# Attend pass of a Performer block: four numerator products gathered at the next group's head, over two banks and two sets of features

## The reference

```
pq  = exp(proj - sq - stab) / sqrt(m) + 1e-06      # features of q
kv  = einsum('bhsm,bhsk->bhmk', pk, v)
z   = sum(pk, axis=2)
num = einsum('bhsm,bhmk->bhsk', pq, kv)
den = einsum('bhsm,bhm->bhs', pq, z)
out = num / den[..., None]
out = out.transpose(...).reshape(...) @ wo
```

## Time and profile before

| | us |
|---|---|
| median of 3 runs | 3307.4 (3306.03 to 3308.24) |
| the profiled execution | 3309.45 |
| its span | 3307.6 |
| PE busy in the span | 3246.5 (98%) |
| DVE, ACT, POOL busy | 2279.7, 1657.2, 1086.0 |
| numerator products L1356, 2048 matmuls | 138.8 busy |
| feature products L1338 and L1344 | 44.3 + 41.2 and 61.4 busy |

### The profile page before, as it was taken

How to read it: one execution, slowest core, us unless ns; L and a number is a source line. 1 busy time by engine, 2 the same in 40 slices (tenths; PEclk the granted TensorE clock), 3 DMA queues, 4 the chain that set the end, 5 groups by cost and what they waited for, 6 DMA issues and landing times.

```text
span 3307.6 us, 73559 instructions
## 1 busy us (share of the span) xinstructions
PE 3246.5 (98%) x28521; PEld 2826.8 (85%) x28521; DVE 2279.7 (69%) x4678; ACT 1657.2 (50%) x3552; POOL 1086.0 (33%) x857
## 2 busy tenths in 40 slices
PE   7999999998899999999999999999999999999998
PEld 6777777777677777777777789999999999999998
DVE  6777777777567667676676666666666676676666
ACT  5666666666454545454545454443444443444443
POOL 3555554555355656565656430000000000000000
PEclk9999999999999999999999999999999999999999
DMA  3222222223344443434434463444444444444443
GB/s 122 95 87 76 102 87 86 95 87 95 105 103 120 109 122 100 129 92 126 111 108 117 137 223 133 146 150 150 147 153 147 151 143 153 139 139 142 150 147 128
DMA packets 250121, 409.60 MB, mean 124 GB/s; under 512 B 94512, under 2 KB 119600, under 8 KB 249776
## 3 DMA queue, kind: packets, MB, share of 16 engines
q1 hardware_dynamic: 249776, 404.90, 38.1%
HBM read 292.50 MB, written 112.33 MB: 122 GB/s over the span
## 4 chain that ended last, share of the span: by engine, by line
PE 72%; DVE 1%; issue 0%; POOL 0%; DMA 0%; ACT 0%; SPq 0%; DVEq 0%; POOLq 0%; ACTq 0%
PE ffn_hidden L188 32%; PE attend_gated L188 22%; PE ffn_result L188 8%; PE attend_num L1356 4%; PE attend_feat L1320 2%; PE attend_feat L1338 2%; PE ffn_turn L1803 1%; PE attend_feat L1344 1%; PE attend_turn L1328 0%; DVE ffn_yb L1770 0%; DMA den_d<-attend_raw 0%; DVE attend_top L1255 0%; DVE attend_below_parts L1268 0%; DVE attend_below_parts L1266 0%; POOL shared_y L1163 0%
## 5 line engine op out<-in xcount | busy, mean ns | idle before, releaser
L188 PE MATMUL ffn_hidden<-ffn_yT_hi,ffn_wa_hi 128*128 128x256 f32 x2048 | 574.1, 280 | 4.9 <-DVE ffn_wa_lo L1691 2.9
L188 PE MATMUL ffn_hidden<-ffn_yT_lo,ffn_wa_hi 128*128 128x256 f32 x2048 | 573.3, 280 | 0.0
L188 PE MATMUL ffn_hidden<-ffn_yT_hi,ffn_wa_lo 128*128 128x256 f32 x2048 | 572.1, 279 | 0.0
L329 POOL TENSOR_TENSOR ffn_n_rstd<-ffn_n_base,ffn_n_power 128x2 f32<-128x2 f32 x32 | 27.5, 860 | 1299.4 <-DVE ffn_n_negmean L324 1299.4
L188 PEld LDWEIGHTS ffn_hidden<-ffn_yT_hi,ffn_wa_hi 128*128 128x128 f32 x2048 | 385.0, 188 | 5.9 <-DVE ffn_wa_lo L1691 3.6
L188 PEld LDWEIGHTS ffn_hidden<-ffn_yT_hi,ffn_wa_lo 128*128 128x128 f32 x2048 | 385.2, 188 | 0.0
L188 PEld LDWEIGHTS ffn_hidden<-ffn_yT_lo,ffn_wa_hi 128*128 128x128 f32 x2048 | 384.9, 188 | 0.2
L1673 ACT ACTIVATE ffn_ht_hi<-ffn_hs 128x512 fp32r<-128x512 f32 x248 | 156.7, 632 | 409.9 <-DVE ffn_hs L1720 409.9
L1724 DVE TENSOR_TENSOR ffn_ht_lo<-ffn_hs,ffn_ht_hi 128x512 fp32r<-128x512 f32 x248 | 173.6, 700 | 219.2 <-ACT ffn_ht_hi L1673 219.2
L698 ACT ACTIVATE keys_e<-keys_feat,keys_below 128x128 f32<-128x128 f32 x1024 | 283.3, 412 | 54.6 <-DVE keys_below L763 54.6
L633 POOL TENSOR_TENSOR keys_z_sum<-keys_z_sum,keys_e 128x512 f32<-128x512 f32 x192 | 243.7, 1287 | 189.9 <-ACT keys_e L698 189.7
(11 more groups left out here) (274 smaller groups left out, 9560.7 us busy)
## 6 DMA issues: line engine op xcount, KB each, us to landing
ffn_tq<-part_d SPq DMA_DIRECT2D x248, 512.0 KB, 4.0
keys_xin<-in_L_attn_x_dram SPq DMA_DIRECT2D x32, 512.0 KB, 4.2
xn_d<-keys_xn SPq DMA_DIRECT2D x32, 512.0 KB, 2.8
xT_d<-keys_xT_whole SPq DMA_DIRECT2D x32, 512.0 KB, 2.6
u_d<-keys_uq_turned SPq DMA_DIRECT2D x32, 512.0 KB, 2.9
shared_xTf<-xT_d SPq DMA_DIRECT2D x32, 512.0 KB, 5.3
r_d<-shared_gate SPq DMA_DIRECT2D x32, 512.0 KB, 3.1
attend_o<-rden_d SPq DMA_DIRECT2D x128, 128.0 KB, 2.7
```

Source lines behind the costliest of these rows:

```text
L188: last = pe.matmul(out, stationary[a], moving[b], start=start and n == 0, stop=stop and n == len(TERMS) - 1)
```

## The change

The four `num` jobs of a group leave the body (where 0, 1 and 2 stood behind `feat` 1, `out` 1 and `wo` 1, and 3 behind the next `max` 0) and stand together at the head of the next group's body, on PE and on ACT. Chunks 0 and 2 go to bank `num`, 1 and 3 to bank `turn`, which otherwise holds the turned `below`. The features of `hi` 1 get tiles of their own, `pT_late`, and `hi` goes ahead of `out` 1 on DVE. In `feat` the four products with `belowT` of the first chunk go behind the second chunk's plain ones. The crossing lists change alike.

```diff
-        pT = [sb(f"pT{j}_hi", [P, 2 * GT]) for j in range(HC)]
+        pT_late = sb("pT_late", [P, HC, 2 * GT])
+        pT = [[sb(f"pT{j}_hi", [P, 2 * GT]) for j in range(HC)], [pT_late[:, j, :] for j in range(HC)]]
...
+        num_bank = [num.t, turn]
...
-        PE_BODY = [("max", 0, 0), ("num", 3, -1), ("k", 0, 0), ("max", 1, 0), ("k", 1, 0), ("r", 0, 0),
...
+        PE_BODY = [("num", 0, -1), ("num", 1, -1), ("num", 2, -1), ("num", 3, -1), ("max", 0, 0), ("k", 0, 0),
...
-                act.activation(raw[:, n, :], num.t[:, :], ACT.Copy).then_inc(num.free, 1)
+                act.activation(raw[:, n, :], num_bank[n % 2][:, :], ACT.Copy).then_inc(num.free, 1)
...
-                        wait(dve, num.full, NC * g + 2 * n)
-                        dve.tensor_scalar(pT[j][:, :], feat[j].t[:, :], FLOOR, None, ALU.add).then_inc(feat[j].free, 1)
+                        wait(dve, num.full, NC * (g - 1) + 2 * n + 2)
+                        dve.tensor_scalar(pT[n][j][:, :], feat[j].t[:, :], FLOOR, None, ALU.add).then_inc(feat[j].free, 1)
...
                 if job == "below":
-                    wait(pe, belowT_ready, g)
+                    wait(pe, num.free, NC * g)
...
                 if job == "feat":
                     for c in range(2):
-                        cols = slice(c * GT, (c + 1) * GT)
                         for j in range(HC):
-                            pe.matmul(feat[j].t[:, cols], omT[rows(j), :], qT[g % 2][rows(j), 2 * n + c, :], start=True, stop=False)
-                        if c == 0 and n == 0:
-                            pe.wait_ge(belowT_ready, g + 1)
...
+                            pe.matmul(feat[j].t[:, c * GT:(c + 1) * GT], omT[rows(j), :], qT[g % 2][rows(j), 2 * n + c, :],
+                                      start=c == 0, stop=False)
+                    pe.wait_ge(belowT_ready, g + 1)
...
+                    for c in range(2):
                         for j in range(HC):
-                            last = pe.matmul(feat[j].t[:, cols], pick[rows(j), 2 * n + c, :], belowT[rows(j), :],
-                                             start=False, stop=True)
+                            last = pe.matmul(feat[j].t[:, c * GT:(c + 1) * GT], pick[rows(j), 2 * n + c, :],
+                                             belowT[rows(j), :], start=False, stop=c == 1)
...
                 if job == "num":
-                        pe.wait_ge(kvz_ready, 2 * b + 2)
-                    wait(pe, num.free, NC * g + n)
+                        pe.wait_ge(kvz_ready, 2 * (g // GB) + 2)
+                    if n == 1:
+                        pe.wait_ge(belowT_ready, g + 1)
+                    wait(pe, num.free, NC * g + n - 1)
...
-                            last = pe.matmul(num.t[rows(j), part * GT:(part + 1) * GT],
+                            last = pe.matmul(num_bank[n % 2][rows(j), part * GT:(part + 1) * GT],
...
-                                             pT[j][:, n % 2 * GT:(n % 2 + 1) * GT], start=True, stop=True)
+                                             pT[n // 2][j][:, n % 2 * GT:(n % 2 + 1) * GT], start=True, stop=True)
```

More of the change, by code:

```diff
@@ L1015, in attend_pass @@
         y_ready, gained, offsets, y_stored = sem("y_ready"), sem("gained"), sem("offsets"), sem("y_stored")
-        PE_BODY = [("max", 0, 0), ("num", 3, -1), ("k", 0, 0), ("max", 1, 0), ("k", 1, 0), ("r", 0, 0),
-                   ("below", 0, 0), ("feat", 0, 0), ("r", 1, 0), ("out", 0, 0), ("feat", 1, 0),
-                   ("num", 0, 0), ("out", 1, 0), ("num", 1, 0), ("wo", 0, -1), ("wo", 1, -1),
-                   ("num", 2, 0)]
-        DVE_BODY = [("top", 0, 0), ("top", 1, 0), ("recip", 0, -1), ("below", 0, 0), ("mix", 0, 1), ("exp", 0, 0), ("o", 0, -1), ("out", 0, 0),
-                    ("out", 1, 0), ("mix", 1, 1), ("hi", 1, 0), ("wo", 0, -1), ("wo", 1, -1),
-                    ("stats", 0, -1),
-                   ("part_lo", 0, 0)]
-        ACT_BODY = [("num", 3, -1), ("norm", 0, -2), ("k", 0, 0), ("k", 1, 0), ("below", 0, 0), ("kv", 0, 0),
-                    ("r", 0, 0), ("exp", 0, 0), ("mix", 0, 1), ("r", 1, 0), ("oT", 0, -1),
-                    ("num", 0, 0), ("exp", 1, 0), ("num", 1, 0), ("mix", 1, 1), ("num", 2, 0),
-                   ("part_hi", 0, 0)]
+        PE_BODY = [("num", 0, -1), ("num", 1, -1), ("num", 2, -1), ("num", 3, -1), ("max", 0, 0), ("k", 0, 0),
+                   ("max", 1, 0), ("k", 1, 0), ("r", 0, 0), ("below", 0, 0), ("feat", 0, 0), ("r", 1, 0), ("out", 0, 0),
+                   ("feat", 1, 0), ("out", 1, 0), ("wo", 0, -1), ("wo", 1, -1)]
+        DVE_BODY = [("top", 0, 0), ("top", 1, 0), ("recip", 0, -1), ("below", 0, 0), ("mix", 0, 1), ("exp", 0, 0),
+                    ("o", 0, -1), ("out", 0, 0), ("hi", 1, 0), ("out", 1, 0), ("mix", 1, 1), ("wo", 0, -1),
+                    ("wo", 1, -1), ("stats", 0, -1), ("part_lo", 0, 0)]
+        ACT_BODY = [("num", 0, -1), ("num", 1, -1), ("num", 2, -1), ("num", 3, -1), ("norm", 0, -2), ("k", 0, 0),
+                    ("k", 1, 0), ("below", 0, 0), ("kv", 0, 0), ("r", 0, 0), ("exp", 0, 0), ("mix", 0, 1), ("r", 1, 0),
+                    ("oT", 0, -1), ("exp", 1, 0), ("mix", 1, 1), ("part_hi", 0, 0)]
         POOL_BODY = [("diff", 0, 1), ("k", 0, 0), ("k", 1, 0), ("norm", 0, -2), ("mix", 0, 1), ("oT", 0, -1),
@@ L1866, in feed_forward_pass @@
         return Programs(sync, gpsimd, scalar, vector, tensor, mem), y_loaded, stored
-PE_CROSSING = (("attend", "max", 0, -1), ("attend", "num", 3, -2), ("attend", "k", 0, -1), ("attend", "max", 1, -1),
-               ("attend", "k", 1, -1), ("attend", "r", 0, -1), ("attend", "below", 0, -1), ("attend", "feat", 0, -1),
-               ("attend", "r", 1, -1), ("attend", "out", 0, -1), ("attend", "num", 0, -1), ("attend", "out", 1, -1),
-               ("attend", "feat", 1, -1), ("attend", "num", 1, -1), ("attend", "wo", 0, -2), ("attend", "num", 2, -1),
-               ("attend", "wo", 1, -2), ("attend", "num", 3, -1), ("ffn", "turn", 0, 0), ("ffn", "w1", 0, 0),
+PE_CROSSING = (("attend", "num", 0, -2), ("attend", "num", 1, -2), ("attend", "num", 2, -2), ("attend", "num", 3, -2),
+               ("attend", "max", 0, -1), ("attend", "k", 0, -1), ("attend", "max", 1, -1), ("attend", "k", 1, -1),
+               ("attend", "r", 0, -1), ("attend", "below", 0, -1), ("attend", "feat", 0, -1), ("attend", "r", 1, -1),
+               ("attend", "out", 0, -1), ("attend", "feat", 1, -1), ("attend", "out", 1, -1), ("attend", "wo", 0, -2),
+               ("attend", "wo", 1, -2), ("attend", "num", 0, -1), ("attend", "num", 1, -1), ("attend", "num", 2, -1),
+               ("attend", "num", 3, -1), ("ffn", "turn", 0, 0), ("ffn", "w1", 0, 0),
                ("ffn", "w1", 1, 0), ("ffn", "w1", 2, 0), ("ffn", "w2", 0, 0), ("ffn", "w2", 1, 0),
@@ L1880 @@
                 ("attend", "below", 0, -1), ("attend", "exp", 0, -1), ("attend", "o", 0, -2),
-                ("attend", "out", 0, -1), ("attend", "out", 1, -1), ("attend", "hi", 1, -1), ("attend", "wo", 0, -2),
+                ("attend", "out", 0, -1), ("attend", "hi", 1, -1), ("attend", "out", 1, -1), ("attend", "wo", 0, -2),
                 ("ffn", "weights", 0, 0), ("attend", "wo", 1, -2), ("attend", "stats", 0, -2), ("ffn", "turn", 0, 0),
```

15 lines of the change are left out of this document (8 added, 7 removed), and 2 rows, old and new, of the table KEYS_OVER.

## The result

The changed kernel takes 3288.27 us in the median of its runs (3284.26 to 3290.12), the kernel before 3307.01 beside it (3306.03 to 3308.24): a ratio of 0.9942 with a 95% interval of 0.9927 to 0.9957. That is 18.7 us less. 3287.0 was predicted.

The account below looks back on a forecast made before the run. The prediction took PE's own work as the bound. It summed 12 us from 30 periods, 4.5 from group 0 and 3.5 from the end to 20 us, forecasting a median of 3287 us (own case 3279 to 3297, range 3270 to 3306).

Parts of the forecast that it names:

- PE's sum: PE's work per group: numerators and `max` 0 0.60 less, `feat` 0.10 less, 0.05 lost on banks; 0.65 us saved.
- the ring: Two numerator banks at the head: `num` 2 waits for ACT's copy to free its bank, 0.05 us lost a group.
- The wait for `oT_lo`: PE at `wo` 0 waits for POOL's `oT_lo`: 0.35 us plus 0.10 restart a group, leaving a gain of 0.20.
- all behind it on POOL end about 0.25 later: With `feat` 0 faster, DVE's `o` goes first and delays POOL's `y` product and its later queue by about 0.25 us.
- The irregular groups: Every fourth group POOL makes `part` and meets DVE; the longer head gives POOL 1.6 us: 30 x 0.19 = 5.7 gained.
- Group 0: First attend group: 1.5 us less waiting for second features and 3.2 us of half clock avoided; 4.5 us counted.
- The end: Last group and feed-forward start: no wait for `below` (1.3 us), weights split earlier on ACT; 3.5 us gained.
- the 4.75: Sign at a group's head on PE: 4.75 us from the first numerator to `k` 0.
- Full gain: Rival: POOL's queue ends before PE arrives at `wo` 0, so no wait; 3274 us, chance 0.20.
- Collisions: Rival: DVE against POOL makes the `wo` 0 wait about 0.9 and irregular groups stay; 3302 to 3310, chance 0.17.
- `hi` against `oT_lo`: Rival: a piece of DVE's `hi` (0.62 us) holds POOL's `oT_lo` up in each group; 3305 us, chance 0.05.
- Slower through ACT: Rival: ACT's copies come late to the head and PE waits 1.2 us at `num` 2; 3323 us, chance 0.08.

Follow-up runs that it names:

- the last experiment: Repeat of the changed kernel with POOL's `oT_lo` put ahead of `mix_lo` 0: 3274.37 us, ratio 0.9901 to the kernel before.
- `oT_lo` first: The changed kernel with two POOL jobs exchanged, `oT_lo` ahead of `mix_lo` 0: 3274.94 us, ratio 0.9902 to the kernel before.
- its own run: The changed kernel with `hi` moved back behind `out` 1 and `mix` 1 on DVE: 3288.36 us, ratio 0.9941 to the kernel before.

## Why the prediction was right, and where not

The time lies 1.3 us from the forecast, by the mechanism that it named. That it is so close is in part luck: the runs of this kernel lie 6 us apart, and the profiled pair differs by 25.1 us where 20 were forecast. Point by point:

- **PE's sum, 0.65 a group with the ring's 0.05: confirmed, a little low.** With POOL's wait removed the period is 0.68 less. 0.08 to 0.10 of that is `feat`. The ring shows no step of 0.05 ahead of the third job; instead each numerator job takes 0.02 to 0.03 more than its streaming, from what cause no run separates.
- **The wait for `oT_lo`, 0.35 and 0.10 for the restart: the mechanism is right, the size was off.** PE arrives at 14.33, as forecast. The wait is 0.21 to 0.31 and the slow start of the first matmul behind it 0.11. The net gain of a regular period was 0.28, and 0.35 where the wait is shortest, not 0.20. The step that failed is "all behind it on POOL end about 0.25 later": `o` came first as forecast (1.22 instead of 2.30) and `y` was held up (2.32), but then `mix_lo` no longer met `o` and took 2.37 instead of 3.35. One hold-up took the place of the other, and `oT_lo` ends only 0.07 later. In the groups in which `o` still comes second (2.30, with `mix_lo` 3.36; one in four) it ends at 14.49, as before.
- **The irregular groups, 5.7 us: right in the sum, and in the cause for 4.1 of it.** From group 2 on all periods are within 0.14 of each other now. Moving POOL's `part` alone, in the kernel before, gives 4.1 us, and a shorter head brings the collision back and a later `part` takes it away again. The other 1.5 belong to the groups with `part_lo`, which the prediction put down to POOL as well. They go with the longer head (32.27 there as elsewhere), but not with the late `part`: the rows point to DVE's `part_lo` instead, and that is not tested.
- **The sum for the 30 periods** was 12 and is 14.5: some 30 x 0.29 = 8.7, and 5.7 for the irregular ones.
- **Group 0, 4.5 us: 5.9.** (The two parts of the forecast, 1.5 and 3.2, make 4.7.) The wait fell to 2.1 instead of 2.6 and the half clock is gone. These are PE and ACT there:

```profile
866.34 1.05 PE L1357 MATMUL attend_turn<-attend_pT_hi,attend_kvz_hi 128*32 128x256 f32 x16
...
869.46 1.07 PE L1357 MATMUL attend_num<-attend_pT_late,attend_kvz_hi 128*32 128x256 f32 x16 [2.07 <-ACT attend_raw L1185]
```

```profile
867.87 1.06 ACT L1195 ACTIVATE attend_mix_hi<-shared_mixed 128x1024 fp32r<-128x1024 f32 x1 [3.27 <-DVE shared_mixed L1241]
868.83 0.58 ACT L1185 ACTIVATE attend_raw<-attend_num 128x512 f32<-128x512 f32 x1
```

  ACT has `mix_hi` ahead of the first copy, as I had said. Whether the clock falls behind that wait differs from one execution of the same program to the next, as the last experiment shows, and on the side of the kernel before as well (44.6 us here, 42.2 and 42.3 with the same order of PE elsewhere). So the 5.9 hold for this pair of executions. The median gained 18.7 where the profiled pair gained 25.1: the profiled execution of before lies 2.4 above its median and that of the changed kernel 4.0 below. Of the 25.1 the keys pass gave 2.0; where the rest of the difference lies isn't shown.
- **The end, 3.5 us: 2.8.** Nearly all of it is won before the feed-forward pass begins. These are its first matmuls, before and after, 26.0 and 23.5 behind `r` 0 of group 31:

```profile
1895.37 1.09 PE L1803 MATMUL ffn_turn<-shared_ident,ffn_y_in 128*128 128x128 f32 x8
```

```profile
1870.51 1.09 PE L1804 MATMUL ffn_turn<-shared_ident,ffn_y_in 128*128 128x128 f32 x8
```

  Of these 2.5 us, 1.5 are the late last group of before (`r` 0 to `wo` 0 18.07 instead of 16.54, with the wait of 1.3 for `below`), and 1.0 is the new order in the last group, where PE doesn't wait for `oT_lo` (14.33). The first hidden product is 2.76 earlier, and behind that nothing more is won. The waits of the feed-forward's start fall from 5.7 to 4.8 us in sum (`hT_lo` 2.3 where it was 0.8, the others less), but the changed kernel is granted 0.50 from 1886.0 to 1889.4, where the kernel before had 1.00 at the same place. What the forecast expected of weights split earlier on ACT can't be told from that.
- **The signs.** Of those that the prediction named, the 4.75, both `feat` at 1.3, the wait of group 0 under 3 us and `mix` 0 at 1.7 came as said. The step ahead of the third job didn't. PE's view of waits shows no 10 us for `oT_lo`; the starts give 7.8.
- **The rivals.** Full gain: not in this kernel, but with `oT_lo` first the time is the one that it forecast (3274, measured 3274.94), with 26.1 us from the 30 periods where it had 25.2. Collisions: refuted here, and real as soon as the head is shorter. `hi` against `oT_lo`: refuted by its own run. Slower through ACT: the starts of the four jobs show no stall behind ACT, and `oT_lo` didn't come late enough. What the second set of feature tiles is worth by itself no run shows.
